# One softmax-weighted attention layer's high/low splits regrouped between ScalarE and VectorE, and the router's selection done in fewer instructions

## The reference

```python
# L0 feed-forward, called twice (before and after the attention); 64 experts, 8 chosen
logits = einsum('bsh,he->bse', hidden_states, router_w)
affinity = sigmoid(logits)
top_scores, top_idx = top_k(affinity, 8)
top_w = top_scores / (sum(top_scores, -1, keepdims=True) + 1e-09)
router_mask = einsum('bske,bsk->bse', one_hot(top_idx, 64), top_w)
shared = einsum('bsi,ih->bsh', silu(h @ shared_gate_w) * (h @ shared_up_w), shared_down_w)
return shared + routed          # routed: every expert, weighted by router_mask

# L0 attention, called once; 16 heads of 8 features, queries = keys
y = x.reshape(b, t, 16, 8).transpose(0, 2, 1, 3)
attn = softmax(einsum('bhtk,bhsk->bhts', y, y) / sqrt(8), -1)
o = einsum('bhts,bsc->bhtc', attn, x)            # the values are all 128 features
return o.transpose(0, 2, 1, 3).reshape(b, t, 16 * 128) @ weight
```

## Time and profile before

| what | value |
|---|---|
| median of 3 runs | 2722.59 us |
| profiled execution, device time | 2723.6 us |
| its span, first to last instruction | 2721.8 us |
| mean granted TensorE clock | 0.969 of full |
| heads: from 700 to 1640 us, 940 us | PE 923.95, DVE 907.01, ACT 833.02 us busy |
| first router, chunks in steady state | about 45 to 78 us |
| second router, chunks in steady state | about 1684 to 1726 us |

### The profile page before, as it was taken

One profiled execution on the slowest core, in us unless ns is written; L12 is line 12 of the kernel. 1 busy time (PEld: TensorE's weight loads), 2 busy tenths in 40 slices (PEclk: granted clock), 3 DMA queues, 4 the chain that ended last, 5 costly groups with the idle time before them and its releaser, 6 DMA issues. The chain is left out here.

```text
span 2721.8 us, 35051 instructions
## 1 busy us (share of the span) xinstructions
PE 2542.9 (93%) x11075; PEld 1903.1 (70%) x11075; DVE 2224.0 (82%) x3288; ACT 1821.4 (67%) x3022; POOL 1227.7 (45%) x1258
## 2 busy tenths in 40 slices
PE   7899999996999999999999998899999999788888
PEld 4688888874666666666666665688888886466656
DVE  7787777776999999999999997787777885578665
ACT  4455555556888888888888885355555555567665
POOL 3566666664323333233232322466666663154411
PEclk9999999998999999999999999999999999889899
DMA  3566666645333333333333331566666650000000
GB/s 95 115 144 145 142 136 136 142 98 165 99 106 98 103 106 102 105 101 98 107 104 102 102 93 35 120 144 144 144 138 136 143 128 9 24 24 8 8 8 31
DMA packets 107385, 271.47 MB, mean 100 GB/s; under 512 B 30784, under 2 KB 35648, under 8 KB 107072
## 3 DMA queue, kind: packets, MB, share of 16 engines
q1 hardware_dynamic: 82192, 235.42, 35.2%
q0 software_dynamic: 24576, 33.62, 4.5%
q10 hardware_dynamic: 432, 0.20, 0.0%
HBM read 258.35 MB, written 10.76 MB: 99 GB/s over the span
## 5 line engine op out<-in xcount | busy, mean ns | idle before, releaser
L679 POOL TENSOR_TENSOR moe_experts_lo<-moe_experts_hidden,moe_experts_hi 128x512 fp32r<-128x512 f32 x512 | 662.5, 1294 | 340.0 <-ACT moe_experts_hi L617 339.8
L963 DVE TENSOR_TENSOR heads_e_lo<-heads_e,heads_e_hi 128x1024 fp32r<-128x1024 f32 x512 | 616.2, 1224 | 26.1
L624 ACT ACTIVATE psum<-psum 128x512 f32<-128x512 f32 x512 | 298.0, 582 | 478.8 <-PE psum L90 478.8
L797 POOL DMA_DIRECT2D heads_left<-heads_parts x512 | 307.4, 616 | 671.8 <-PE psum L851 610.6
L903 ACT ACTIVATE heads_e<-psum 128x1024 f32<-128x1024 f32 x512 | 520.7, 1024 | 108.1 <-PE psum L851 108.1
L651 DVE TENSOR_TENSOR moe_experts_weighted<-moe_spread,psum 128x512 f32<-128x512 f32 x512 | 351.3, 686 | 190.5 <-PE psum L90 186.5
L88 PE MATMUL psum<-heads_e_hi,heads_v_lo 128*128 128x512 f32 x1024 | 429.4, 419 | 18.2 <-DVE heads_u L929 18.2
L88 PE MATMUL psum<-moe_n_hi,moe_w_lo 128*128 128x512 f32 x1024 | 400.8, 391 | 5.0 <-PEq L54 4.7
L89 PE MATMUL psum<-heads_e_lo,heads_v_hi 128*128 128x512 f32 x1024 | 404.4, 395 | 0.0
L90 PE MATMUL psum<-heads_e_hi,heads_v_hi 128*128 128x512 f32 x1024 | 400.9, 392 | 0.0
L89 PE MATMUL psum<-moe_n_lo,moe_w_hi 128*128 128x512 f32 x1024 | 400.1, 391 | 0.0
(11 more groups left out here) (403 smaller groups left out, 4083.3 us busy)
## 6 DMA issues: line engine op xcount, KB each, us to landing
moe_spread<-moe_mask SPq DMA_DIRECT2D x128, 1024.0 KB, 10.1
heads_right<-heads_parts SPq DMA_DIRECT2D x512, 64.0 KB
heads_left<-heads_parts POOLq DMA_DIRECT2D x512, 64.0 KB, 2.5
heads_scale<-heads_inverse_copy SPq DMA_DIRECT2D x64, 512.0 KB, 3.7
moe_experts_raw<-in_gate SPq DMA_DIRECT2D x16, 256.0 KB, 11.7
moe_experts_raw<-in_up SPq DMA_DIRECT2D x16, 256.0 KB, 11.9
moe_experts_raw<-in_down SPq DMA_DIRECT2D x16, 256.0 KB, 11.8
heads_parts<-heads_e_hi SPq DMA_DIRECT2D x16, 256.0 KB, 3.2
```

Of the source, the lines that this page charges most:

```text
L624: act.activation(psum[:, GATE + p % 2, :], psum[:, GATE + p % 2, :], ACT.Silu).then_inc(silu_ready, 1)
L679: pool.tensor_tensor(lo[:, p, :], hidden[:, p % 2, :], f(hi[:, p, :]), ALU.subtract).then_inc(low_ready, 1)
L797: eng.dma_start(f(tile[row:row + 2 * HEAD, h % 2, :]), parts_dram[dims, order:order + 2, at]).then_inc(loaded[h % 2], 16)
L963: dve.tensor_tensor(e_lo[:, s, :], e[:, s % 4, :], f(e_hi[:, s, :]), ALU.subtract).then_inc(low, 1)
```

## The change

The attention: DVE's high part of an even tile covers the first 896 of 1024 columns; ACT's instruction after an odd exponential covers the even tile's last 128 columns and the whole odd tile, 1152 columns in one. DVE does the low parts of both tiles after that instruction. The scaled sums `u` are split in one high and one low instruction of 1024 columns in place of two of 512 each; the two reads of the banks OUT stay as they were.

The router: the sum of the chosen is taken from the 8 best by one reduction, the product and the scaling are one instruction each of 256 columns, and the mask is copied out of PSUM by ACT, after the next chunk's affinity.

```diff
                 def step(c, j, last):            # route, ScalarE
                     if not last:
                         affinities(c + 1, 1 - j)
+                    if c > 0:
+                        copy_mask(c - 1, 1 - j)
                     act.wait_ge(up_ready, c + 1)
...
-                    for q in range(4):           # route, VectorE, pick
-                        dve.wait_ge(rest_ready, c * 4 + (q + 1))
-                        dve.scalar_tensor_tensor(out=chosen[:, j, q, :], ..., accum_out=total[:, j, q:q + 1])
+                    dve.tensor_reduce(total[:, j, :], best[:, j, :, :], X, ALU.add).then_inc(total_found, 1)
+                    dve.wait_ge(rest_ready, c * 4 + 4)
+                    dve.scalar_tensor_tensor(out=chosen[:, j, :, :], ...).then_inc(chosen_ready, 1)
...
-                    for q in range(4):
-                        dve.tensor_scalar(routed[:, j, q, :], chosen[:, j, q, :], total[:, j, q:q + 1], None, ALU.mult)
+                    dve.tensor_tensor(routed[:, j, :, :], chosen[:, j, :, :], total (spread over 64), ALU.mult)
...
-                    dve.tensor_copy(mask[:, j, :], psum[0:EXPERTS, MASK, :]).then_inc(mask_ready, 1)
...
-                    for half in range(HALVES):   # heads, ScalarE, u_highs
-                        act.wait_ge(scaled_ready, g * HALVES + half + 1)
-                        act.copy(u_hi[:, g % 2, half, :], u[:, half, :]).then_inc(u_high, 1)
+                    act.wait_ge(scaled_ready, (g + 1) * HALVES)
+                    act.copy(u_hi[:, g % 2, :], u[:, :]).then_inc(u_high, 1)
...
-                        act.copy(e_hi[:, s, :], e[:, s % 4, :]).then_inc(act_high, 1)
+                        both = e[:, s % 4 - 1:s % 4 + 1, :].rearrange("p a b -> p (a b)")
+                        both_hi = e_hi[:, s - 1:s + 1, :].rearrange("p a b -> p (a b)")
+                        act.copy(both_hi[:, T - REACH:], both[:, T - REACH:]).then_inc(act_high, 1)
...
-                    if s in ACT_HIGH:            # heads, VectorE
-                        dve.wait_ge(act_high, high_act)
+                    if s % 2 == 0:
+                        high(h, s)               # columns 0 to T - REACH of tile s, REACH = 128
                     else:
-                        ... tensor_copy(e_hi[:, s, :], e[:, s % 4, :]) and wait for it
-                    dve.tensor_tensor(e_lo[:, s, :], e[:, s % 4, :], f(e_hi[:, s, :]), ALU.subtract)
+                        dve.wait_ge(act_high, highs(h, s)[0])
+                        dve.wait_ge(dve_high, highs(h, s)[1])
+                        for tile in (s - 1, s):
+                            split(h, tile)
                     if s == TRAIL - 1 and h >= 1:
                         scale_sums(h - 1)
```

More of the change, by code:

```diff
@@ L360, in route_and_share @@
         rest_ready, chosen_ready, total_ready, inverse_ready = sem("rest"), sem("chosen"), sem("total"), sem("inverse")
+        total_found = sem("total_found")
         routed_ready, routed_turned, mask_ready = sem("routed"), sem("routed_turned"), sem("mask")
@@ L420, in step @@
                     after(pe, mask_ready, c)
-                    wait_apart(pe, routed_ready, c * 4 + 4, pe_passed)
+                    wait_apart(pe, routed_ready, c + 1, pe_passed)
                     for q in range(4):
@@ L442, in affinities, with copy_mask @@
                     act.activation(affinity[:, j, :], psum[:, LOGITS, :], ACT.Sigmoid).then_inc(affinity_ready, 1)
+                def copy_mask(c, j):
+                    act.wait_ge(routed_turned, c + 1)
+                    after(act, mask_stored[j], 16 * (c // 2))
+                    act.copy(mask[:, j, :], psum[0:EXPERTS, MASK, :]).then_inc(mask_ready, 1)
                 def step(c, j, last):
@@ L456, in _ @@
                 each_chunk(step)
+                copy_mask(CHUNKS - 1, 1)
             @block.vector
@@ L470, in pick @@
                                           in_values=scores(q), imm_value=-1.0).then_inc(rest_ready, 1)
-                    for q in range(4):
-                        dve.wait_ge(rest_ready, c * 4 + (q + 1))
[L473 to L476, removed]
+                    dve.tensor_reduce(total[:, j, :], best[:, j, :, :], mybir.AxisListType.X, ALU.add).then_inc(total_found, 1)
+                    dve.wait_ge(rest_ready, c * 4 + 4)
+                    dve.scalar_tensor_tensor(out=chosen[:, j, :, :], in0=rest[:, j, :, :], scalar=0.0,
+                                             in1=psum[:, TURNED + j, :].rearrange("p (q t) -> p q t", q=4)[:, :, 0:EXPERTS],
+                                             op0=ALU.is_lt, op1=ALU.mult).then_inc(chosen_ready, 1)
+                    dve.wait_ge(total_found, c + 1)
                     dve.tensor_scalar(total[:, j, :], total[:, j, :], 1e-9, 2.0, ALU.add,
@@ L481, in pick @@
                     dve.wait_ge(inverse_ready, c + 1)
-                    for q in range(4):
-                        dve.tensor_scalar(routed[:, j, q, :], chosen[:, j, q, :], total[:, j, q:q + 1], None,
-                                          ALU.mult).then_inc(routed_ready, 1)
+                    dve.wait_ge(chosen_ready, c + 1)
+                    dve.tensor_tensor(routed[:, j, :, :], chosen[:, j, :, :],
+                                      total[:, j, :].unsqueeze(2).to_broadcast([P, 4, EXPERTS]), ALU.mult).then_inc(routed_ready, 1)
                 def leave(c, j):
-                    dve.wait_ge(routed_turned, c + 1)
-                    after(dve, mask_stored[j], 16 * (c // 2))
-                    dve.tensor_copy(mask[:, j, :], psum[0:EXPERTS, MASK, :]).then_inc(mask_ready, 1)
                     dve.wait_ge(down_ready, c + 1)
@@ L758, in head_attention @@
         scale = sb(f"{tag}_scale", [P, 2, T])
-        u = sb(f"{tag}_u", [P, HALVES, BANK])
-        u_hi, u_lo = sb(f"{tag}_u_hi", [P, 2, HALVES, BANK], F32R), sb(f"{tag}_u_lo", [P, 2, HALVES, BANK], F32R)
+        u = sb(f"{tag}_u", [P, T])
+        u_hi, u_lo = sb(f"{tag}_u_hi", [P, 2, T], F32R), sb(f"{tag}_u_lo", [P, 2, T], F32R)
         SCORES, OUT, SUM = 0, 4, 6
@@ L773, in head_attention @@
         ACT_HIGH = (1, 3, 5, 7)
+        REACH = 128
         TRAIL = 6
@@ L831, in add_head @@
                     cols = slice(g % HEADS * P, (g % HEADS + 1) * P)
-                    pe.wait_ge(u_low, (g + 1) * HALVES)
+                    pe.wait_ge(u_low, g + 1)
                     if g % HEADS == 0:
@@ L835, in add_head @@
                     for half in range(HALVES):
+                        at = slice(half * BANK, (half + 1) * BANK)
                         last = product(pe, psum[:, SUM + half, :], (w_hi[:, cols], w_lo[:, cols]),
-                                       (u_hi[:, g % 2, half, :], u_lo[:, g % 2, half, :]),
+                                       (u_hi[:, g % 2, at], u_lo[:, g % 2, at]),
                                        first=g % HEADS == 0, last=g % HEADS == HEADS - 1)
@@ L916, in _, with high, split @@
             def _(dve):
+                def high(h, s):
+                    n, at = h * TILES + s, slice(0, T - REACH)
+                    dve.wait_ge(exp_done, n + 1)
+                    after(dve, out_done, n - (TILES - 1))
+                    if n < BATCH:
+                        dve.wait_ge(copied[n], BATCH_COPIED)
+                    dve.tensor_copy(e_hi[:, s, at], e[:, s % 4, at]).then_inc(dve_high, 1)
+                def split(h, s):
+                    dve.tensor_tensor(e_lo[:, s, :], e[:, s % 4, :], f(e_hi[:, s, :]), ALU.subtract).then_inc(low, 1)
                 def invert(g):
@@ L926, in scale_sums @@
                     dve.wait_ge(out_done, (g + 1) * TILES)
+                    after(dve, u_low, g)
                     for half in range(HALVES):
-                        after(dve, u_low, (g - 1) * HALVES + half + 1)
-                        dve.tensor_tensor(u[:, half, :], scale[:, g % 2, half * BANK:(half + 1) * BANK],
-                                          psum[:, OUT + half, :], ALU.mult).then_inc(scaled_ready, 1)
+                        at = slice(half * BANK, (half + 1) * BANK)
+                        dve.tensor_tensor(u[:, at], scale[:, g % 2, at], psum[:, OUT + half, :], ALU.mult).then_inc(scaled_ready, 1)
                 def u_lows(g):
[L933 to L936, removed]
+                    dve.wait_ge(u_high, g + 1)
+                    dve.tensor_tensor(u_lo[:, g % 2, :], u[:, :], f(u_hi[:, g % 2, :]), ALU.subtract).then_inc(u_low, 1)
                 def add_batch(b):
```

10 lines of the change are left out of this document (1 added, 9 removed).

## The result

The change makes the kernel slower: 2791.75 us median of 4 runs (2788.34 to 2794.13) against 2722.88 us of 4 runs before, a ratio of 1.0255, 95% interval 1.0241 to 1.0269. The forecast was 2796 us, range 2765 to 2816. The profiled execution after has a span of 2792.3 us, 70.5 us more than before.

The account below looks back on a forecast made before the run. PE was taken to bound the heads, held once a head by DVE's read of OUT. 2723.6 + 79.7 (heads) - 6.2 (router) = 2797.1 us for the profiled execution, 2796 us as a median; 8-in-10 range 2765 to 2816.

Parts of the forecast that it names:

- What bounds the heads: Heads: PE sets the pace, held once a head by DVE's late read of OUT, losing about 0.39 of 15.45 us.
- The low part behind ACT's cast, 1.14 us a head: Tiles 4 and 5: the even tile's low part, formerly beside ACT's cast, delays DVE's read of OUT by 1.14 us.
- ACT's growth, 0.11 us: Heads: 128 more columns lengthen ACT's cast by 0.11 us, which adds in the pair of tiles 4 and 5.
- ACT kept ahead of PE: Other pairs of a head: ACT's 0.21 us of idle time covers its 0.11 us growth, leaving 0.10 us.
- DVE's smaller high part and the merged sums: nothing: Heads: DVE's savings, 0.34 us a head at most and 0.15 us a head, were taken as worth 0.
- The sum for the heads, 79.7 us: Heads: 63 x 1.25 = 78.8 us slower, 79.7 with the tail; a head takes 16.7 us.
- the clock: Heads: no loss taken; as rival, longer stalls lower PE's clock, another 1.1 us a head, 2865 us, chance 0.02.
- the single step: End of the heads' stage: sums in single instructions instead of staggered halves cost 0.9 us, once.
- The router, 6.2 us: Two routers: about six steady chunks each gain 0.52 us, 6.2 us in all; bounds 0 and 18 us.
- The chunk of 5.07 us: Router: a chunk falls from 5.59 to 5.07 us, held by PE's down product rather than DVE's 4.5 us.
- the stores do not become the end: Router's end: the earlier mask store keeps stores and spread loads from setting the end; otherwise the gain's bound is 0.
- The wait before the addition: Router chunk: DVE's addition was to wait 0.6 us for PE's down product, a sign of the forecast being right.

Follow-up runs that it names:

- run 4: The full change with ACT's instruction covering the odd tile alone (1024 columns) and DVE's high part 1024: 2785.55 us, 1.023 of the kernel before.
- run 5: The kernel before with only the scaled sums u split in one high and one low instruction: 2723.2 us, 1.0002.
- run 8: The kernel before with DVE's read of OUT between the low parts of tiles 4 and 5 instead of behind both: 2696.05 us, 0.99.
- run 3: The kernel before with only the even tile's low part moved behind the wait for ACT's high part of the odd tile: 2797.44 us, 1.0275.
- run 7: The full change with the read of OUT ahead of tiles 4 and 5's low parts and ACT covering the odd tile alone: 2692.58 us, 0.9888.
- run 1: The kernel before with the attention's part of the change alone, router as before: 2807.07 us, 1.0311.
- the runs with the early read: Runs, on either attention, with DVE's read of OUT ahead of or between the low parts of tiles 4 and 5: 2677.09 to 2696.05 us.
- run 9: The kernel before with the read of OUT between the low parts of tiles 4 and 5, plus the change's router part: 2683.33 us, 0.9855.
- run 10: The full change with the read of OUT ahead of tiles 4 and 5's low parts and SyncE's heads_right loads before the scale traffic: 2680.65 us, 0.9842.
- run 12: The attention before with the read between tiles 4 and 5's low parts, the change's router, and heads_right loads before the scale traffic: 2677.09 us, 0.9844.

## Why the prediction was right

**What bounds the heads.** Right. DVE's occupancy of 96% was no bound; its order was. By the rule of the Trainium skill that the prediction weighed (Perfetto Trace Analysis, Identifying the Most-Contended Engine) the relief of DVE should have paid; runs 4 and 5 show that it paid nothing, and run 8 that the same work of DVE fits in a shorter head.

**The low part behind ACT's cast, 1.14 us a head.** Right: run 3 measures 16.60 against 15.46 us, 1.14. **ACT's growth, 0.11 us.** 0.103 by the cast, 0.10 by the head; ACT kept ahead of PE, as was taken: its next exponential begins 0.11 us after the cast, where 0.10 was forecast. **DVE's smaller high part and the merged sums: nothing.** Right by runs 4, 5 and 7. DVE's idle time before the low parts is 0.49 us and not 0.3, which costs nothing; PE's stall is 1.63 us for about 1.6.

**The sum for the heads, 79.7 us.** The stretch grew by 85.0 and the attention in it by 85.4, so this is the term that was mis-sized, by 5.3 to 5.7. The 63 reads cost 78.7 us for the forecast 78.8, though not evenly: an ordinary head costs 16.70 less 15.46; the first read comes 1.0 us later; in the head after it PE's wait grew from 1.82 to 3.06 us, the clock was at its lower level behind the wait in both kernels, and the interval grew by 2.2 us; the last interval did not grow (12.04 against 12.06 us). What was left out is the clock, which the prediction took as no loss and gave 0.02 as a rival in every head. After the additions to `x` that come once a batch, PE waits 1.97 us in place of 1.47, and in this trace the matmuls behind that wait run at the lower of the two clock levels. The kernel after, from one `add_head` to the `weighted_rows` behind it:

```profile
960.13 0.40 PE L90 MATMUL psum<-heads_u_hi,heads_w_hi 128*128 128x512 f32 x1
962.50 0.47 PE L88 MATMUL psum<-heads_e_hi,heads_v_lo 128*128 128x512 f32 x1 [1.97 <-DVE heads_u L951]
...
963.95 0.62 PE L88 MATMUL psum<-heads_e_hi,heads_v_lo 128*128 128x512 f32 x1
964.37 0.63 PE L89 MATMUL psum<-heads_e_lo,heads_v_hi 128*128 128x512 f32 x1
```

```profile
964.60:967.00 2.40, 2.40 (x9) 1.38 (x8) 2.40 (x3) 0.00 (x0) 0.00 (x0) 0.50 0.05 14
```

Starts are 0.42 us apart in place of 0.23, at a granted clock of 0.50 (1.2 GHz), and that head takes 18.2 us in place of 16.7: 1.5 us, three times. But that wait doesn't drop the clock each time: in the trace of run 1, with the same attention, there are three waits of 1.96 to 1.98 us at the same places and only the last is followed by matmuls at the lower level, and its attention takes 82.5 us more than before in place of 85.4. So 3 of the missing us are not a price of the attention's change alone; why the clock fell behind one wait and not behind the same wait elsewhere is open. The end of the stage costs 2.2 us more in place of 0.9, with the last `add_head` at the lower clock too, after a wait of 2.43 us:

```profile
1735.48 0.79 PE L88 MATMUL psum<-heads_u_hi,heads_w_lo 128*128 128x512 f32 x1 [2.43 <-DVE heads_u_lo L955]
1736.07 0.63 PE L89 MATMUL psum<-heads_u_lo,heads_w_hi 128*128 128x512 f32 x1
```

Of these 2.2 us 0.9 are the single step, as forecast, and 1.3 the clock. That makes 4.5 + 1.3 = 5.8 us of clock that the sum did not have. The warning of the Trainium skill (TensorE: Matmul & The Clock Gate, HAM oscillation), that waits of PE bring it back to its lower clock, came true at these four places and not at the waits of 1.47 us in the ordinary heads.

**The router, 6.2 us.** 3.9 + 3.4 = 7.3 us in the traces. The chunk of 5.07 us came out as worked out, but the way from the chunk to the stage was wrong in part, and the number owes something to luck. The prediction counted six shorter chunks in each router and held that the stores do not become the end. The stores were the end before and are the end after, so chunks behind the second group of spread loads do not count: from the first addition to the issue of those loads the routers gained 2.6 and 2.4 us, from there to the end 0.3 and 0.5, and ahead of the first addition 1.1 and 0.4, where traces of one router code differ by 2.5 us. The wait before the addition is 0.37 us and not 0.6: the small addition behind the 256-column product takes 0.33 us, not 0.17. It starts at 59.32 while that product is shown until 59.40; whether that makes it longer isn't shown.

**The total.** 73.5 us forecast over the median, 68.9 measured. Heads 5.3 above and router 1.1 below the forecast; 7.2 us came off in layers that the change doesn't touch, within the 981.6 to 991.0 us that these layers take in the fourteen traces. That the total came out so near is luck in part: the clock's cost in the attention and the faster execution of those layers nearly cancel.

## What to carry to other kernels

A nearly full engine is not the bound while another engine's regular wait names one instruction of it: ask at what time that instruction runs, not how much work stands on the engine. Work that was done beside a wait costs nothing; moved behind the wait it costs in full where another engine is already waiting for the instruction that follows it, here in one pair of tiles out of four. Before work is shifted between engines, try moving the instruction that frees a buffer up to where its engine idles.

## What the runs showed of the hardware

In the kernel after, PE's clock stayed at its full level through a wait of 1.47 us in every ordinary head of 16.7 us, and was at half behind waits of 1.97 us, three times, and 2.43 us. The length of the wait alone does not settle it. In run 1 the clock stayed at full behind two of three waits of 1.97 us, in run 3 behind two of three of 2.04 us, and in run 5 behind one of 2.43 us; in the kernel before it was at half behind a wait of 1.82 us, in the second head.

Times from read to read below 15.03 us are not shorter heads. In the runs with the early read single ones took 14.47 to 14.73 us, nearly all in the few heads behind a read that came late, as in run 8 behind the additions to `x` (16.04, then 14.73 us): the next reads catch up. Taken from PE's first `add_head` matmul to the next, no head of any run takes under 14.95 us but the last, and PE is busy for 898.1 us of 900 in run 8 and over 899 in runs 9, 10 and 12. So some 15.0 us a head is as fast as PE goes in these kernels.

An ACT cast costs 0.80 to 0.85 ns a column (617, 1054 and 1157 ns for 512, 1024 and 1152 columns), a DVE cast from SBUF 0.52 (616 and 682 ns for 896 and 1024).
